# A DLRM tower on one core: whole-table one-hot tiles, two look-up banks, divided copies, and a step in two parts

## The reference

```python
e = jnp.stack([tbl_0[ids[:, 0]], ..., tbl_25[ids[:, 25]]], axis=1)      # tables of 1000 to 125000 rows
combined = jnp.concatenate([dense_features[:, None, :], e], axis=1)     # [2048, 27, 128]
interactions = jnp.einsum('bnd,bmd->bnm', combined, combined)
z = jnp.concatenate([dense_features, interactions[:, _TRIU_I, _TRIU_J]], axis=1)
h = jnp.concatenate([z, dense_features], axis=1)                        # 607 columns
h = jnp.maximum(h @ W_top1 + b_top1, 0.0)                               # 512
h = jnp.maximum(h @ W_top2 + b_top2, 0.0)                               # 256
y = h @ W_top3                                                          # 1
```

## Time and profile before

| | us |
|---|---|
| median of 3 runs | 602.59 (599.72 to 607.67) |
| the profiled execution, device time | 605.72 |
| its span, first to last instruction | 603.9 |
| PE busy / DVE / ACT / POOL | 433.2 / 263.3 / 207.4 / 253.8 |
| mean granted clock of PE | 0.82 |

### The profile page before, as it was taken

The page is one execution under the profiler, slowest core; times in us unless marked ns, Lnnn a source line. Parts: engine busy times, 40 slices in busy tenths (PEclk is TensorE's granted clock), DMA queues, the critical chain, the costliest instruction groups (busy, mean ns, idle before and its releaser), DMA issues.

```text
span 603.9 us, 13994 instructions
## 1 busy us (share of the span) xinstructions
PE 433.2 (72%) x6369; PEld 389.7 (65%) x6369; DVE 263.3 (44%) x258; ACT 207.4 (34%) x313; POOL 253.8 (42%) x261
## 2 busy tenths in 40 slices
PE   3773277766788677787778778786777867787927
PEld 3672157655767667676667767675676766777827
DVE  5981035671544424535244434554154442465221
ACT  3550023443313333234222433233332333335713
POOL 7787545374423445154351644345433344500000
PEclk9886557987868788888787888896887878889978
DMA  8923113031102111031110311121111211101010
GB/s 202 243 55 104 39 32 99 21 108 37 27 25 83 45 33 41 18 92 33 27 45 16 101 34 27 37 86 47 29 26 29 85 42 33 41 7 58 4 58 1
DMA packets 21909, 32.79 MB, mean 54 GB/s; under 512 B 8030, under 2 KB 14846, under 8 KB 21850
## 3 DMA queue, kind: packets, MB, share of 16 engines
q0 software_dynamic: 8288, 16.83, 11.0%
q1 hardware_dynamic: 13562, 15.06, 8.8%
HBM read 28.24 MB, written 3.68 MB: 53 GB/s over the span
## 4 chain that ended last, share of the span: by engine, by line
PE 56%; issue 16%; DVE 12%; ACT 9%; another core or an unknown queue 6%; DMA 1%; SPq 0%; DVEq 0%
PE hot_ps L617 23%; PE gram_ps L642 11%; DVE one_hot L503 9%; PE mlp_ps L649 6%; PE transpose_ps L593 5%; PE mlp_ps L650 5%; PE mlp_ps L651 5%; ACT embed_t L424 4%; ACT embed_t L379 3%; PE hot_ids_ps L599 2%; DVE packed_lo L507 1%; DVE units L489 1%; DMA bounce<-units 1%; DMA rows<-bounce 1%
## 5 line engine op out<-in xcount | busy, mean ns | idle before, releaser
L351 POOL DMA_INDIRECT rows<-table,ids_sb x256 | 252.9, 988 | 272.9 <-PE transpose_ps L593 199.4
L617 PE MATMUL hot_ps<-one_hot,table_hi 125*128 125x256 f32 x640 | 200.2, 338 | 65.7 <-ACT embed_t L424 43.6
L503 DVE TENSOR_TENSOR one_hot<-hot_ids_ps,row_numbers_sb 125x1024 fp32r<-125x1024 f32 x160 | 192.4, 1236 | 110.9 <-PE hot_ids_ps L599 59.4
L617 PEld LDWEIGHTS hot_ps<-one_hot,table_hi 125*128 125x128 f32 x640 | 142.2, 222 | 81.3 <-DVE one_hot L503 46.0
L617 PE MATMUL hot_ps<-one_hot,table_lo 125*128 125x256 f32 x640 | 185.4, 315 | 0.0
L617 PEld LDWEIGHTS hot_ps<-one_hot,table_lo 125*128 125x128 f32 x640 | 143.5, 224 | 0.0
L642 PE MATMUL gram_ps<-embed_t 128*27 128x27 f32 x4096 | 77.3, 205 | 67.0 <-issue 66.1
L642 PEld LDWEIGHTS gram_ps<-embed_t 128*27 128x27 f32 x4096 | 58.8, 117 | 88.2 <-issue 85.3
L379 ACT COPY embed_t<-transpose_ps 128x512 f32<-128x512 f32 (+1 forms) x80 | 85.3, 1066 | 79.9 <-PE transpose_ps L593 51.1
L424 ACT COPY embed_t<-hot_ps 128x256 f32<-128x256 f32 x80 | 54.8, 684 | 148.2 <-PE hot_ps L617 82.1
L489 DVE COPY_PREDICATED units<-late_sb,gram_ps 128x208 f32<-128x208 int32 x32 | 35.1, 1098 | 121.2 <-ACT units L418 115.3
(11 more groups left out here) (49 smaller groups left out, 314.6 us busy)
## 6 DMA issues: line engine op xcount, KB each, us to landing
rows<-table,ids_sb POOLq DMA_INDIRECT x256
embed_t<-table SPq DMA_DIRECT2D x8, 448.0 KB
bounce<-units SPq DMA_DIRECT2D x8, 448.0 KB
scratch<-bounce SPq DMA_DIRECT2D x7, 378.0 KB
rows<-dense SPq DMA_DIRECT2D x16, 64.0 KB
scratch<-table SPq DMA_DIRECT2D x2, 448.0 KB
scratch<-w SPq DMA_DIRECT2D x1, 512.0 KB
scratch<-w_units SPq DMA_DIRECT2D x2, 252.0 KB
```

What stands on the lines that cost most here:

```text
L351: nc.gpsimd.indirect_dma_start(rows[:, t2, f, :], None, tables[table], bass.IndirectOffsetOnAxis(ids_sb[:, slot, table:table + 1], 0)).the ...
L503: nc.vector.tensor_tensor(one_hot[:, n % RING], ids_over, numbers_over, ALU.is_equal).then_inc(one_hot_ready, 1)
L617: last = nc.tensor.matmul(hot_ps[:, 0:GROUP], table[:, k % HOT, step, :], one_hot[:, (2 * k + half) % RING, j, :], start=(step == 0 and ta ...
```

## The change

One-hots become whole tables: ten tiles of 8 by 256 a group in a ring of two in place of twenty of 4 by 256 in a ring of three. `H0` to `H9` are now whole tables of 16 matmuls. The ids of two tables are broadcast at once, 512 columns. Even tables are multiplied into `hot_ps`, odd ones into the second bank of `mlp_ps`, which odd MLP steps use too. Of the transposed banks of a tile, those with odd number (`Q1`, `Q3`) are copied by DVE, the others by ACT. The step lists have the gram products, the MLP and the transposes first and the look-ups at the end: four tables after the first tile, six after the second. The dense weights are loaded behind the second layer's, and `hidden2` lies partly in `scratch`.

The diff, cut to its core:

```diff
-RING = 3
-AHEAD = 2
+RING = 2
+PAIR = 2
+PAIRS = HOT // PAIR
+PAIR_ROWS = PAIRS * GROUPS
 HALF = N // 2
...
@@ -93,16 +94,16 @@
 STEPS = [
-    "D0 S0 M0 G0 Q0 G1 M1 G2 Q1 W0 M2 G3 H0 M3 H1 Q2 H2 W1 H3 Q3 H4 H5 W2 Q4 H6 H7".split(),
-    "G0 H8 G1 H9 Q0 H10 G2 H11 M4 G3 H12 Q1 H13 W3 M5 H14 Q2 H15 W4 M6 H16 Q3 H17 W5 Q4 H18 H19".split(),
+    "D0 S0 M0 G0 G1 Q0 M1 Q1 G2 G3 M2 W0 Q2 W1 M3 Q3 W2 M4 Q4 H0 H1 H2 W3 H3".split(),
+    "G0 G1 Q0 M5 Q1 G2 G3 M6 Q2 W4 Q3 W5 Q4 H4 H5 H6 H7 H8 H9".split(),
 ]
 LAST_STEPS = [
-    "D0 S0 M0 G0 Q0 G1 M1 G2 Q1 M2 G3 M3 Q2 M4 M5 Q3 M6 Q4".split(),
+    "D0 S0 M0 G0 G1 M1 G2 G3 M2 M3 Q0 M4 Q1 M5 Q2 M6 Q3 Q4".split(),
     "G0 G1 G2 G3".split(),
 ]
-FIRST_STEPS = "H0 H1 H2 Q0 H3 H4 H5 H6 Q1 H7 H8 H9 H10 Q2 H11 H12 H13 H14 Q3 H15 H16 H17 Q4 H18 H19".split()
+FIRST_STEPS = "H0 Q0 H1 H2 Q1 H3 H4 Q2 H5 H6 Q3 H7 H8 Q4 H9".split()
...
         last_packed_raw = by_chunk(rows[0:UNIT_P, 0, 0:2 * CHUNKS, :].rearrange("p c d -> p (c d)"))
         y_rows = scratch[0:TILE_COUNT, 0, 0:P]
+        hidden2 = [hidden2_first[:, :], scratch[:, CHUNKS, :]]
...
         raw_tables = [places[k % RAW_PLACES].rearrange("p (j d) -> p j d", d=P) for k in range(HOT)]
         landing = [scratch[:, 0:2, :].rearrange("p c b -> p (c b)"), scratch[:, 2:4, :].rearrange("p c b -> p (c b)"),
                    units[:, 1].rearrange("p k q -> p (k q)")[:, 0:H1]]
-        w1a_sb = landing[2]
+        w1d_sb, w1a_sb = landing[0], landing[1]
         transpose_ps = ps("transpose_ps", [P, 2, PER_BANK, P])
...
             return gram_ps[:, i % 2, 0:ROUND_BLOCKS * N].rearrange("p (q m) -> p q m", m=N)[:, :, first:last]
+        def hot_bank(k):
+            return hot_ps[:, 0:GROUP] if k % 2 == 0 else mlp_ps[:, 1, 0:GROUP]
+        def even_copies(tiles, u):
+            return tiles * EVEN_BANKS + (u + 1) // 2
+        def odd_copies(tiles, u):
+            return tiles * ODD_BANKS + u // 2
+        def embed_source(t2, u):
+            return transpose_ps[:, (t2 * TILE_BANKS + u) % 2, 0:len(features(u)), :]
+        def embed_target(g, t2, u):
+            f = features(u)
+            return embed_t[:, embed_slot(g, t2), :, f[0]:f[-1] + 1].rearrange("p b n -> p n b")
         def unit_slot(buf, r, first, last):
...
@@ -294,10 +317,12 @@
                     sp.wait_ge(weights_lo, CHUNKS)
                     sp.dma_start(scratch[:, :, :], w2.rearrange("(c p) h -> p c h", p=P)).then_inc(weights_loaded, 16)
+                    sp.wait_ge(weights_lo, CHUNKS + 1)
+                    sp.dma_start(w1d_sb, w1_dense).then_inc(weights_loaded, 16)
                     sp.dma_start(w1a_sb, w1_again).then_inc(weights_loaded, 16)
-                    sp.wait_ge(weights_lo, CHUNKS + 1)
-                    sp.wait_ge(w1_summed, 1)
+                    sp.wait_ge(weights_lo, len(pieces))
                 pack(g, buf, landing)
             load_ids(0, 0)
...
@@ -368,15 +392,12 @@
         def _(act):
             def embed_copy(g, buf, t2, u):
-                use = t2 * TILE_BANKS + u
                 if u == 0 and t2 == 1 and g >= 1:
                     act.wait_ge(dense_split_lo, g)
-                act.wait_ge(transposed, TRANSPOSE_USES * g + use + 1)
-                f = features(u)
-                out = embed_t[:, embed_slot(g, t2), :, f[0]:f[-1] + 1].rearrange("p b n -> p n b")
-                nc.scalar.copy(out, transpose_ps[:, use % 2, 0:len(f), :]).then_inc(embed_copied, 1)
+                act.wait_ge(transposed, TRANSPOSE_USES * g + t2 * TILE_BANKS + u + 1)
+                nc.scalar.copy(embed_target(g, t2, u), embed_source(t2, u)).then_inc(even_copied, 1)
             def mlp_copy(g, buf, m):
...
@@ -419,19 +440,19 @@
             def hot_copy(g, k, buf):
-                act.wait_ge(hot_ready, LOOKUPS * g + 2 * (k + 1))
+                act.wait_ge(hot_ready, HOT * g + k + 1)
                 out = over_group(g, HOT_FEATURE + k)
-                nc.scalar.copy(out, hot_ps[:, 0:GROUP].rearrange("p (t b) -> p t b", t=TILES)).then_inc(hot_copied, 1)
+                nc.scalar.copy(out, hot_bank(HOT * g + k).rearrange("p (t b) -> p t b", t=TILES)).then_inc(hot_copied, 1)
             def group(g, buf, steps, mlp_before=True):
                 for t2 in range(TILES):
                     for step, n in [(x[0], int(x[1:])) for x in steps[t2]]:
                         if step == "G" and n % PARTS == PARTS - 1:
                             late_columns(g, buf, t2 * TILE_ROUNDS + n // PARTS)
-                        elif step == "Q":
+                        elif step == "Q" and n % 2 == 0:
                             embed_copy(*next_tile(g, buf, t2), n)
-                        elif step == "H" and n % 2 == 1:
-                            hot_copy(g + 1, n // 2, 1 - buf)
+                        elif step == "H":
+                            hot_copy(g + 1, n, 1 - buf)
                         elif step == "D" and mlp_before:
                             dense_upper(g - 1)
...
@@ -489,18 +510,22 @@
                 nc.vector.copy_predicated(unit_slot(buf, r, 1, UNITS), rows_taken, gram_slot(r, 0, HALF)).then_inc(
                     early_copied, 1)
-            def make_one_hot(n):
-                k, half = n // 2, n % 2
-                if n >= RING:
-                    dve.wait_ge(hot_ready, n - RING + 1)
-                if half == 0:
-                    dve.wait_ge(hot_ids_ready, k + 1)
-                steps = slice(half * HALF_STEPS, (half + 1) * HALF_STEPS)
-                ids_over = hot_ids_ps[0:HOT_P, None, 0:GROUP].to_broadcast([HOT_P, HALF_STEPS, GROUP])
-                numbers_over = row_numbers_sb[:, steps, None].to_broadcast([HOT_P, HALF_STEPS, GROUP])
-                nc.vector.tensor_tensor(one_hot[:, n % RING], ids_over, numbers_over, ALU.is_equal).then_inc(one_hot_ready, 1)
+            def make_one_hot(k):
+                if k >= RING:
+                    dve.wait_ge(hot_ready, k - RING + 1)
+                if k % PAIR == 0:
+                    dve.wait_ge(hot_ids_ready, k // PAIR + 1)
+                ids = hot_ids_ps[0:HOT_P, None, k % PAIR * GROUP:(k % PAIR + 1) * GROUP]
+                nc.vector.tensor_tensor(one_hot[:, k % RING], ids.to_broadcast([HOT_P, HOT_STEPS, GROUP]),
+                                        row_numbers_sb[:, :, None].to_broadcast([HOT_P, HOT_STEPS, GROUP]),
+                                        ALU.is_equal).then_inc(one_hot_ready, 1)
+            def embed_copy(g, buf, t2, u):
+                dve.wait_ge(transposed, TRANSPOSE_USES * g + t2 * TILE_BANKS + u + 1)
+                nc.vector.tensor_copy(embed_target(g, t2, u), embed_source(t2, u)).then_inc(odd_copied, 1)
             def lower(whole, hi, lo):
...
                     pe.wait_ge(dense_loaded[t2], 16 * (g + 1))
                 pe.wait_ge(gathered[t2][u], 16 * len(gathers(u)) * (g + 1))
-                if not (first and use < 2):
-                    pe.wait_ge(embed_copied, TRANSPOSE_USES * g + use - 1)
+                if u >= 2 or not first:
+                    done, at = (TILES * g + t2, u - 2) if u >= 2 else (TILES * g + t2 - 1, u - 2 + TILE_BANKS)
+                    if at % 2 == 0:
+                        pe.wait_ge(even_copied, even_copies(done, at + 1))
+                    else:
+                        pe.wait_ge(odd_copied, odd_copies(done, at + 1))
                 for i, f in enumerate(features(u)):
                     last = nc.tensor.transpose(transpose_ps[:, use % 2, i, :], rows[:, t2, f, :], identity_sb[:, :])
                 last.then_inc(transposed, 1)
...
-            def broadcast_ids(k):
-                row = k % HOT * GROUPS + k // HOT
-                nc.tensor.matmul(hot_ids_ps[0:HOT_P, 0:GROUP],
-                                 selector[:, row:row + 1].to_broadcast([HOT * GROUPS, HOT_P]), hot_ids_sb[:, :],
+            def broadcast_ids(pair):
+                row = pair % PAIRS * GROUPS + pair // PAIRS
+                nc.tensor.matmul(hot_ids_ps[0:HOT_P, :],
+                                 selector[:, row:row + 1].to_broadcast([PAIR_ROWS, HOT_P]), hot_ids_sb[:, :],
                                  start=True, stop=True).then_inc(hot_ids_ready, 1)
             def look_up(g, n):
-                k, half = g * HOT + n // 2, n % 2
-                pe.wait_ge(one_hot_ready, 2 * k + half + 1)
-                if half == 0 and g == 0:
-                    pe.wait_ge(lo_split, k + 1)
-                if half == 0 and k >= 1:
-                    pe.wait_ge(hot_copied, k)
-                for j in range(HALF_STEPS):
-                    step = half * HALF_STEPS + j
+                k = g * HOT + n
+                pe.wait_ge(one_hot_ready, k + 1)
+                if g == 0:
+                    pe.wait_ge(lo_split, n + 1)
+                if k % PAIR == PAIR - 1 and k + 1 < GROUPS * HOT:
+                    broadcast_ids(k // PAIR + 1)
+                if k >= 2:
+                    pe.wait_ge(hot_copied, k - 1)
+                if k % 2 == 1 and odd_bank["stages"]:
```

(14 more changed lines are left out.)

61 lines of the change are left out of this document (33 added, 28 removed).

## The result

The changed kernel takes 651.7 us (649.7 to 656.1) where the kernel before takes 603.9 (599.7 to 607.7): a ratio of 1.086, 95% interval 1.080 to 1.091. It is slower by 8.6%, where 586 us was forecast.

A forecast was written before the change was run, and what follows sets the result against it. No engine is full; hand-overs between TensorE, VectorE and ScalarE bound the kernel. First group 135, five groups 346.5, group 6 60.9 and last group 44.9 give 587.3, plus 1.8 less 3.1 is 586 us; range of 8 in 10, 560 to 622.

The forecast's parts named there:

- Both effects of the gathers: Beside POOL's gathers, gram products drip, and in long gather runs engines see signals late; TensorE loses 7 us a group to these.
- Late signals: Look-up trains standing in nine-gather runs: half of the 7.4 us a group lost if late as today, taken as 3.7.
- on time: Trains without late signals: 9.5 us for four tables, 14.7 for six; as a rival 563 us, chance 0.24.
- late as today: Rival: train signals as late as before, 4.1 and 3.3 us lost, group of 73.0; 609 us, chance 0.26.
- The midway value: TensorE issue rate in trains, 13 a us, between 16 with late signals and 9 with timely ones; half the loss taken.
- The first group, 135: Start to the next group's G0: grams wait for gathers in either order, 133 to 137 us, taken as 135.
- Gram products: G2 and G3 of each half drip until seven gathers end: 8.2 us a pair, 19.4 a group against 15.
- The wait at a group's start: From a group's last look-up to the next M0, waiting for the last look-up copy: 2.5 us as now.
- MLP stages and transposes: M and Q steps between grams and trains: MLP steps 1.4 or 2.6 us, four transposes 0.4 or 0.8.
- the gather runs of seven and nine: POOL in each half: seven gathers after Q0 and Q1, 10.0 us; nine after Q2 to Q4, 11.3 us.
- The ring of two: Rival: late signals in the train of six delay both following one-hots, 10.4 us lost a group; 624 us, chance 0.12.
- The clock rival: Rival: one-hot waits in trains drop TensorE to 1.2 GHz, a pair 7.1 instead of 5.2 us; 622 us, chance 0.08.

The follow-up runs named there:

- E5: The changed kernel with no edit, run in a quick place (kernel before 431.0 us): 452.6 us, ratio 1.040 to the kernel before.
- E11: Changed kernel with the old order of a step and both splits of the next MLP's inputs moved earlier, slow place: 586.0 us, ratio 0.979 to the kernel before.
- E16: E11 without the gathers of tiles 4 to 15, in a slow place: 452.4 us where the kernel before takes 613.3, ratio 0.739.
- E9: Changed kernel with both splits of the next MLP's inputs moved before look-ups 4 and 7 of the group ahead, quick place: 425.2 us, ratio 0.989.
- E10: Kernel before with both splits of the next MLP's inputs moved before look-ups 13 and 19, quick place: 416.6 us, ratio 0.974.
- E12: Changed kernel without the gathers of tiles 4 to 15, quick place: 443.5 us, ratio 1.030 to the kernel before.
- E17: The kernel of E11 again, with all its gathers, in a quick place: 419.6 us where the kernel before takes 434.9, ratio 0.967.
- E1: Changed kernel with the old order of a step put back, whole tiles and two banks kept, quick place: 441.2 us, ratio 1.027 to the kernel before.
- E15: Same edit as E10 (kernel before with early splits), run again in a quick place: 417.4 us, ratio 0.969.
- E18: Same edit as E10 (kernel before with early splits), run again in a quick place: 418.1 us, ratio 0.966.
- E2: Kernel before with only the new order of a step, half tiles and one bank kept, quick place: 468.7 us, ratio 1.090.
- E13: Kernel before without the gathers of tiles 4 to 15, quick place: 430.0 us, ratio 0.999.

## Why the prediction was wrong, point by point

Both effects of the gathers in the slow place were read rightly and are in the trace after. What failed is the price: nearly each term of the sum that they enter was too small, and what the old order covers was not in the sum at all.

**Late signals, 3.7 us a group: the largest single step that failed.** The train of four took 14.0 us (on time 9.5) and the train of six 18.7 (357.65 to 376.3; on time 15.8): 7.4 us lost a group, the size of the rival "late as today". The midway value came from a rate: about 9 TensorE instructions a us in the first 47 us, with signals on time. After the change TensorE issues 4 a us in the same stretch (95 matmuls and 95 loads in 47 us), and signals are later there than anywhere in the kernel before. So a low rate doesn't keep them on time, and half had no ground. The 3.7 us a group that were missing make about 20 of the 65 us missed. They undo the gain that was forecast; that the kernel got slower takes the terms below as well.

**The first group, 135: it took 145.3.** I had taken its signals for on time, since they were so before. After, they were the latest of all. The last matmul of the fourth table starts at 28.20, and ScalarE's copy comes so:

```profile
46.78 0.67 ACT L445 COPY embed_t<-mlp_ps 128x256 f32<-128x256 f32 x1 [18.18 <-remote]
```

Group 0's first gram product moved from 47.9 to 78.3 us. Its first pair then went out at once (128 matmuls in 1.26 us), where in the kernel before the first pair dripped from 47.9 to 75 us; so about 20 of the 30 us were given back. In the quick place of E5 the first product stands at 49.0. In E11 and E16, slow places, it stands at 80.9 and 72.3: the late start comes again there, and the order of `STEPS`, which is the old one in both, isn't its cause. Why the same gathers delay signals in this stretch after the change and not before it stays open: tiles, banks, broadcasts, matmuls per signal and `FIRST_STEPS` changed at once, and no run in a slow place took them apart.

**Gram products, 10.4 us from Q0 to the end of G3: 12.2** (305.67 to 317.85, and 341.19 to 353.35). They do not end 1 us after the last gather; 54 were left, and these and M2 behind them ran at the lower clock. Twice 1.8 a group. The walk set its 19.4 us of gram steps against "15 now"; the eight steps of the old group 3 add up to 16.7.

**The wait at a group's start, "as now 2.5": 3.4** (376.20 to 379.63). It was taken over without asking what the change puts before it: making one-hots two whole tiles ahead sets a second one-hot before VectorE's dense split. E9 against E10 shows the cost.

**MLP stages and transposes** held nearly (7.65 us against 7.8 from M2 to Q4, 4.3 against 3.5 from M6 to Q4), and so did the gather runs of seven and nine. VectorE's transpose copy, taken at 0.9 us, is 1.19, and TensorE doesn't wait for it in group 3.

**The sum again.** The terms above give a group of 69.3 + 3.7 + 3.5 + 0.9 + 1.0 = 78.4 us, and 78.3 is measured; the 1.0 are M6 and the transposes behind it (0.8) and smaller differences. The five steady groups took 392.3 us in place of 346.5. These 45.8 us, the first group's +10.3, group 6's +3.1 and the last's +1.3 are the 60.5 us between 587.3 and the span of 647.8. The rest of the miss is the step from the span to the median: 1.3 us were taken off, and the median lies 3.9 above the span.

**The rivals.** The ring of two (624 us) came nearest and named what binds: idle of 2.68 us on a one-hot, but the price was 7.4 and not 10.4 us a group, so its nearness is luck. The clock rival of 622 us didn't come as told: matmuls in the train of four stayed 0.12 us apart until a stop of 2.68 us, and fell to 0.21 only after it (333.14); in the train of six a stop of 1.88 us (371.75) brought no fall. Read as a rule, what the Trainium skill says in "TensorE: Matmul & The Clock Gate", section "A second HAM failure mode: psum-queue depth-cycling", of one kernel that cycled through PSUM banks would have made the trains swing by themselves; in E12's group 3 the trains of the quick place lose no clock, and the low one follows the 3.17 us stop at the group's head. In E5's group 4 the train of six begins at 0.21, behind M6's narrow matmuls and a wait of 0.91 us, but it comes up to 0.12 while the banks alternate.

**What was left out of the sum altogether** is that the change costs time where no gather or late signal plays a part: 17 us in the quick place (E5). The head of a group is half of it. The other half is the order: with whole tiles, two banks and early splits the new order stands at 0.989 (E9) and the old one at 0.967 (E17). The old order covers many hand-overs with a gram product or an MLP stage; the prediction priced those of the trains one by one, and never priced what the old order hid. Of the 44 us of span, some 14 to 17 are of this kind if the quick place is a guide; the rest comes with the gathers.

## What to carry over

Before a long instruction is made longer on an engine, list what stands behind it in that engine's queue at the point where another engine waits. Here one more 2.3 us tile ahead of a 0.6 us split is what whole tiles cost in the old order (10 us in E1, nothing once the split was moved), and moving the split was worth 3% in the kernel before (E10, E15, E18: 417 us against 431) and 5% in the changed one. Each look-up needs a hand-over; in a train it stands in the open, and interleaved with independent products much of it is covered (51.0 us of waits in E2, 27.6 in E13). The version to use is the kernel before with early splits, or the whole tiles in the old order with them: E17 and E18 can't be told apart in a quick place, and in a slow one only the second was seen (E11, 0.979 of before). In both the units' split still stands ahead of the last look-up only, and PE waits for it, in E17's steady groups 1.86 us each:

```profile
236.81 0.39 PE L687 MATMUL mlp_ps<-packed_hi,w1u_hi 126*128 126x256 f32 x1 [1.86 <-DVE packed_lo L532]
```
